# Attention layers: query and key projections earlier in periods 1, 2, 4 and 5, and another order of the weight splits where the two layers meet

## What is computed

```
x  = layernorm(x * s1)
q  = (x Wq^T) * qdc      k = (x Wk^T) * kdc      v = (x Wv^T) * vdc * s2
out  = softmax(q k^T / sqrt(32)) v          # 16 heads of 32, 128 tokens
y    = (out Ww^T) * wdc + (v Wu^T) * udc    # "W": output product, "U": skip product
dc[b, o] = 1 / sqrt(sum_i W[o, i]^2 s[b, i]^2 + 1e-8)
```

## Time and profile before

| | us |
|---|---|
| median of 3 runs | 4036.56 |
| lowest, highest | 4034.94, 4038.31 |
| profiled execution | 4034.65 |
| its span | 4032.3 |
| mean granted TensorE clock | 0.954 |

### The profile page before, as it was taken

One profiled execution on the slowest core, in us unless ns is written; L12 is line 12 of the kernel. 1 busy time (PEld: TensorE's weight loads), 2 busy tenths in 40 slices (PEclk: granted clock), 3 DMA queues, 4 the chain that ended last, 5 costly groups with the idle time before them and its releaser, 6 DMA issues. The chain is left out here.

```text
span 4032.3 us, 63692 instructions
## 1 busy us (share of the span) xinstructions
PE 3744.9 (93%) x22068; PEld 2296.2 (57%) x22068; DVE 3030.6 (75%) x3176; ACT 1335.1 (33%) x2014; POOL 1886.6 (47%) x1446
## 2 busy tenths in 40 slices
PE   8999759999998789999999999988999759999999
PEld 6777513333433567777767777756777513434344
DVE  4766679999996667777777777744666669999997
ACT  3555401111111444343434444323555401111111
POOL 2655635555553123344454444342555635555554
PEclk9999859999999799999999999998999959999999
DMA  3666755565654323222322222223666755556563
GB/s 121 241 239 239 298 178 167 179 194 173 196 176 125 101 87 122 79 81 81 106 87 90 79 79 79 66 80 116 229 240 246 271 189 166 189 179 194 172 193 120
DMA packets 272123, 630.17 MB, mean 156 GB/s; under 512 B 33216, under 2 KB 35904, under 8 KB 271840
## 3 DMA queue, kind: packets, MB, share of 16 engines
q1 hardware_dynamic: 267568, 619.03, 46.1%
q10 hardware_dynamic: 4352, 8.39, 0.6%
HBM read 390.87 MB, written 241.70 MB: 157 GB/s over the span
## 5 line engine op out<-in xcount | busy, mean ns | idle before, releaser
L1156 DVE CUSTOM_DVE_ANT_0 l3r_g<-l3r_g,l3r_pv,l3r_cf 128x1024 f32<-128x1024 f32 x512 | 674.5, 1339 | 70.8 <-PE l3r_pv L962 48.2
L1156 DVE CUSTOM_DVE_ANT_0 l0r_g<-l0r_g,l0r_pv,l0r_cf 128x1024 f32<-128x1024 f32 x512 | 674.1, 1339 | 69.4 <-PE l0r_pv L962 48.0
L102 PE MATMUL l1h_ps_p<-l1h_xh,l1c_wh 128*128 128x512 f32 x768 | 324.0, 422 | 9.2 <-POOL l1c_wl L2159 4.7
L104 PE MATMUL l1h_ps_p<-l1h_xl,l1c_wh 128*128 128x512 f32 x768 | 309.0, 402 | 0.0
L2120 POOL TENSOR_TENSOR l1h_st<-l1h_veps 128x1 f32<-128x1 f32 x64 | 35.4, 554 | 582.1 <-DVE l1h_veps L1983 582.1
L103 PE MATMUL l1h_ps_p<-l1h_xh,l1c_wl 128*128 128x512 f32 x768 | 306.5, 399 | 0.0
L974 PE MATMUL l3r_py<-l3r_g,l3r_cd 128*32 128x512 f32 x2048 | 283.0, 627 | 0.1
L962 PE MATMUL l0r_pv<-l0r_x,l0r_wv 32*128 32x512 f32 x1024 | 260.9, 508 | 23.2 <-POOL l0r_wv L882 15.6
L962 PEld LDWEIGHTS l3r_pv<-l3r_x,l3r_wv 32*128 32x128 f32 x1024 | 97.5, 188 | 324.4 <-issue 204.5
L962 PE MATMUL l3r_pv<-l3r_x,l3r_wv 32*128 32x512 f32 x1024 | 262.4, 512 | 21.1 <-POOL l3r_wv L882 15.8
L962 PEld LDWEIGHTS l0r_pv<-l0r_x,l0r_wv 32*128 32x128 f32 x1024 | 96.8, 186 | 324.2 <-issue 204.3
(11 more groups left out here) (386 smaller groups left out, 9038.4 us busy)
## 6 DMA issues: line engine op xcount, KB each, us to landing
l0r_x<-xhl_s SPq DMA_DIRECT2D x128, 512.0 KB, 11.7
l3r_x<-xhl_s SPq DMA_DIRECT2D x128, 512.0 KB, 11.2
xhl_s<-l0a_xo SPq DMA_DIRECT2D x116, 512.0 KB, 4.6
xhl_s<-l3a_xo SPq DMA_DIRECT2D x116, 512.0 KB, 4.6
gate_s<-l0a_gate SPq DMA_DIRECT2D x64, 256.0 KB, 2.7
l0r_dx<-dx_s SPq DMA_DIRECT2D x32, 512.0 KB, 13.3
l0r_gate<-gate_s SPq DMA_DIRECT2D x32, 512.0 KB, 13.9
l0r_crow<-feed_s SPq DMA_DIRECT2D x64, 256.0 KB
```

The lines of the kernel that those rows point to most:

```text
L102: pe.matmul(out, wh, xh, start=first, stop=False)
L104: return pe.matmul(out, wh, xl, start=False, stop=last)
L1156: dve._custom_dve(bass.dve_ops.TENSOR_ADD_SAT, out=g[:, t, j, :], in0=g[:, (t - 1) % TS, j, :], in1=pv[j % 2][:, :], s0=cf[:, q, t, 0, j:j ...
```

## The change

In periods 1 and 2 TensorE now does the Q projection ahead of values 0 (where U stands in later periods) and the K projection between turn 1 and values 1 (where W stands). In periods 4 and 5, where U exists, Q goes between turn 1 and values 1 and K stays. `jobs` lists the new order, so that the banks follow. VectorE's keep_q and ScalarE's keep_k move forward with them. Period 3, a burst, and all other periods keep their order.

In period 31 ScalarE makes the high half of K ahead of a normalise and of X2, and that of V ahead of the high halves of v and o. GpSimd makes the low half of K ahead of the low halves of v and o, and that of V ahead of the addition of W and the scaling of x.

```diff
--- before.py
+++ after.py
@@ -1341,9 +1341,17 @@
 
         def jobs(p):
             names = BURST if p.mod(4) == 3 else PLAIN
+            if extra(p) and p.off < 3:
+                return ("Q", "K", "S", "T", "V", "U", "W")
+            if extra(p) and p.off > 3:
+                return ("U", "Q", "S", "K", "T", "V", "W")
             if extra(p):
                 names = names[:-3] + ("Q", "S", "K", "T", "V")
             return names
+
+        def sooner(p, job):
+
+            return extra(p) and p.off != 3 and (p.off < 3 or job == "Q")
 
         def bank(p, name):
 
@@ -1662,19 +1670,27 @@
                 if p.is_at(0):
                     sum_rows(3)
                     sum_rows(4)
+                if sooner(p, "K"):
+                    project(p, Q, "Q", q_mm)
                 values(g, 0)
                 turn(g, 1)
                 if burst:
                     turn_x(p, "X3")
                 mix_w(p)
+                if sooner(p, "K"):
+                    project(p, K, "K", k_mm)
+                elif sooner(p, "Q"):
+                    project(p, Q, "Q", q_mm)
                 values(g, 1)
                 turn(g, 2)
-                project(p, Q, "Q", q_mm)
+                if not sooner(p, "Q"):
+                    project(p, Q, "Q", q_mm)
                 if extra(p):
                     next_sum_rows(p)
                 values(g, 2)
                 turn(g, 3)
-                project(p, K, "K", k_mm)
+                if not sooner(p, "K"):
+                    project(p, K, "K", k_mm)
                 if extra(p):
                     next_add_rows(p)
                 values(g, 3)
@@ -1787,10 +1803,10 @@
                 keep_pt(g, 0)
                 if burst:
                     high_x(p, "X1")
+                    if p.is_at(B - 1):
+                        high_swap(K)
                     normalise(p.plus(4))
                     high_x(p, "X2")
-                if p.is_at(B - 1):
-                    high_swap(K)
                 exponent(p, 0)
                 for m in range(5):
                     if p.is_at(m + 1):
@@ -1818,17 +1834,20 @@
                     take_root(root, skip, 3)
                     high_weight(3)
                     square_weight(3)
+                if p.is_at(B - 1):
+                    high_swap(V)
                 high_v(p.plus(-3))
                 high_o(p.plus(-5))
-                if p.is_at(B - 1):
-                    high_swap(V)
+                if sooner(p, "K"):
+                    keep_k(p)
                 keep_pt(g, 2)
                 keep_pt(g, 3)
                 if p.is_at(B + 3):
                     high_swap(U)
                 if p.is_at(B + 5):
                     high_swap(W)
-                keep_k(p)
+                if not sooner(p, "K"):
+                    keep_k(p)
                 keep_o(g)
                 keep_v(p)
                 if p.is_at(-1):
@@ -2052,6 +2071,8 @@
                 if burst:
                     low_x(p, "X1")
                 centre(p, 0)
+                if sooner(p, "K"):
+                    keep_q(p)
                 scale_u(p)
                 if burst:
                     low_x(p, "X2")
@@ -2067,6 +2088,8 @@
                 if burst:
                     low_x(p, "X3")
                 scale_w(p)
+                if sooner(p, "Q") and not sooner(p, "K"):
+                    keep_q(p)
                 if p.is_at(-1):
                     pair_factor()
                     keep_skip()
@@ -2082,7 +2105,8 @@
                 if p.is_at(B - 1):
                     low_swap(Q)
                 share(p, 0)
-                keep_q(p)
+                if not sooner(p, "Q"):
+                    keep_q(p)
                 if extra(p):
                     spill_next(p)
                 if p.is_at(4):
@@ -2169,14 +2193,14 @@
             def period(p):
                 factors(p.plus(4))
                 add_u(p.plus(-4))
+                if p.is_at(B - 1):
+                    low_swap(K)
                 low_v(p.plus(-3))
                 low_o(p.plus(-5))
                 if p.is_at(B - 1):
-                    low_swap(K)
+                    low_swap(V)
                 add_w(p.plus(-6))
                 scale_x(p.plus(5))
-                if p.is_at(B - 1):
-                    low_swap(V)
 
             periods(pool, LEAD, TAIL, period)
```

## The result

The changed kernel takes 4014.16 us (median of 13 runs, 4009.23 to 4023.29) against 4033.06 us (13 runs, 4023.07 to 4038.31) for the kernel before on the same chips: a ratio of 0.9958, 95% interval 0.995 to 0.9965, or 17 us less (14 to 20). The profiled execution took 4014.11 us, its span is 4011.8 us. Runs of one kernel spread over 14 to 15 us here, so stretches of a trace say more about single steps than totals do. The two profiled executions differ by more than the ratio says, by 20.5 us (4034.65 to 4014.11); 16.6 of them lie between period 1's scores and the phase's last scores, and the rest outside, where the change touches nothing.

What follows compares the result with a forecast made beforehand. TensorE, busy 93% of the span, was taken as the bound, losing time only to waits and the lower clock. Wins of 5.4 + 2.8 + 0.3 + 1.4 + 5.0 = 14.9 us off 4036.56 gave 4021.7 us, range 4014 to 4029.

Steps and rivals of the forecast that it cites:

- The stands: Periods 1, 2, 4, 5: TensorE's 4.76 us waits ahead of values 1 go in periods 1 and 2; others remain, up to 3.0.
- The clock's charge: Periods 1 and 2: 0.5 and 1.3 us added for TensorE running at the lower clock after the new stands.
- Period 5: Falls from 25.50 to 24.1 us: stands of 3.0 and 1.4, plus 1.4 for the lower clock; 1.4 won.
- The sum: Periods 1, 2, 4, 5 and the joint: 5.4 + 2.8 + 0.3 + 1.4 + 5.0 = 14.9 us won.
- The joint: Period 31: three waits become one of some 3.5 us ahead of Q; stretch 27.4 us, 5.0 won (1.5 to 6.5).
- Rival 2: Joint: GpSimd keeps the port through its next two copies, so little is won there; 4025.2 us, chance 0.13.
- Costed at nothing: Period 3's kept order, bank waits in periods 4 to 6, keep_q and SyncE's loads: each 0, or 0.5 us at most.
- Rival 1: Early periods: the waits only move and the clock is lost again, giving 3 us for 9.9; 4028.6 us, chance 0.12.
- Rival 3: Early periods: several short stands each bring back the lower clock, making the kernel slower, 4045 us at 120 matmuls; chance 0.03.
- the sign of 0.85: Early periods: clocks under 0.85 there would show the forecast wrong.
- Rival 4: All changed periods: the clock stays up everywhere, 21.3 us won, 4015.3 us; chance 0.07.

Runs made afterwards that it cites:

- three queue experiments: Changed kernel with one move each: VectorE's period 2 row factors later (4013.02 us), ScalarE's period 4 square root later (4008.11), next layer's row factors earlier (4008.31).
- early kernel: Changed kernel with the joint's orders of ScalarE and GpSimd put back, so only periods 1, 2, 4 and 5 change: 4022.93 us, ratio 0.9971.
- repeat: The changed kernel once more, unaltered: 4013.53 us (1 run).
- root: Changed kernel with ScalarE's square root of period 4 behind pt 2 (its copy for values 2) instead of ahead: 4008.11 us (1 run).
- next row factors: Changed kernel with the next layer's row factors on VectorE behind period 4's second share instead of at its end: 4008.31 us (1 run).
- low Q moved: Changed kernel with VectorE's low Q at the joint right behind X2's low half, before GpSimd's low K: 4015.14 us (1 run).
- low Q and low V moved: Changed kernel with VectorE's low Q behind X2's low half and GpSimd's low V right behind low K: 4010.64 us (1 run).
- all five moves: Changed kernel with period 2 row factors, square root and next row factors moved, low Q first, low V behind low K: 4002.46 us, ratio 0.9927.
- GpSimd alone: Kernel before with only GpSimd's two moved splits at the joint, ScalarE in its old order: 4036.16 us (1 run); joint 27.04 us.

## Why the prediction was right, step by step

- **The stands.** Right: values 1 without a stand in periods 1 and 2; 2.56 (2.7 forecast) ahead of T in period 2; 2.35 (2.65) ahead of values 2 in period 4; 2.86 (3.0) ahead of values 1 in period 5. The short ones were put too high: 1.2 ahead of values 2 in periods 1 and 2 was 0.58 in each, and 0.7 ahead of T in period 1 was 0.51. The three queue experiments show the causes of the long ones. TensorE's work without waits was put too low: 15.3 us in period 1, where it was busy for 15.86, and 18.3 in period 4, where it was busy for 18.57 at the full clock. The two errors nearly cancel. (The forecast's sums take 1.8 us for the two stands of period 1 and 3.95 for those of period 2, where their terms add up to 1.9 and 3.9.)
- **The clock's charge** is the term that was mis-sized most. 0.5 and 1.3 us were put on periods 1 and 2; in the profiled execution they lost nothing. Of the six other profiles with period 2's order unaltered, five (the early kernel, the repeat, and those with root, next row factors or low Q moved) put period 2 at 21.0 to 22.0, and only the one with low Q and low V moved at 19.45. So for period 2 the charge was a fair mean, and the profiled execution was lucky. Period 1 took 16.94 to 16.96 us in every profile of the new order: its 0.5 was wrong.
- **Period 5** was charged twice, for a second stand of 1.4 and for the lower clock. The lower clock stretched turn 2 and S (1.94 us for a busy 1.07) just where TensorE would have stood, and no stand was left: 22.85 in place of 24.1. The 24.1 would have been met by other terms: in the two executions in which period 4 had kept the full clock with its stand of 2.35, the lower one lasted in period 5 into the key projection, and the period took 24.00 and 24.04 us (0.86), without a second stand.
- **The sum.** Over periods 1 to 5 the new order took 105.96 to 109.44 us in the five profiles that have it unaltered (the change, its repeat, the early kernel and the two with low Q moved), mean 107.30, and the old one 119.11 to 119.85 in four, mean 119.38: 12.1 us won on average, where 9.9 were forecast. The joint's order gives 26.69 on average where 27.4 was forecast. Against the 32.42 before, the two averages add up to 17.8 us, inside the 14 to 20 measured. So the forecast was short by about 2 us in the early periods and 0.7 at the joint.
- **The joint.** Right in mechanism and nearly in size (27.4 forecast; 25.69 to 27.71 in the six profiles that have its order unaltered): one wait of 3.5, low Q of 3.70, low V ended ahead of V. In the changed kernel's profile the lower clock lasted through Q, 5.26 us where 4.5 were put, and left K at the full one, where 0.6 were put. Rival 2 (GpSimd keeps the port) is out: when low K ended at 2002.94, VectorE, which had been waiting, went first, and GpSimd's low half of v, 1.27 us alone, took 3.34. GpSimd's order alone is worth 5.4 (32.42 - 27.04), ScalarE's 0.3.
- **Costed at nothing.** Period 3 took 24.31 us for 24.14 (its second stand is 2.54 for 2.17), and period 7 25.47 for 24.03, by a lower clock behind an unchanged stand of 2.50 (0.93 for 1.00). Of the 18.2 won in five stretches 16.6 are left between period 1's scores and the phase's last ones (1265.4 us for 1282.0).
- **Rival 1** (the waits only move) holds for period 4 alone, 0.2 won, and there only with the lower clock: at the full one the same order won 1.75 (22.66 - 20.91).
- **Rival 3** (slower by the clock) is out: the worst of the five profiles above still won 9.7 us in periods 1 to 5 (119.11 - 109.44). That one has the only clock under the sign of 0.85 in a period that the change touches, 0.84 in period 2 (21.99 us), 2.5 us more than at the full level; in the changed kernel's own two profiles no early period is under 0.92.
- **Rival 4** (the clock stays up everywhere, 4015.3 us) has the number nearest to the measured one, by chance: its mechanism did not hold. The clock was 0.92 in period 4, 0.93 in period 5 and 0.88 at the joint.

## What to carry to other kernels

Where an engine in strict order stands behind another's queue, work put into the hole wins the hole, and the next stand is read from the same queue's next entries; here the long ones could be told to 0.3 us, the short ones to 0.6. Before moving an operation of GpSimd with two SBUF operands forward, list which ones of VectorE will be queued against it, since each waited for the other whole here (3.70 us for 2.28, 6.66 for 4.5). Filling a pause of some 2 to 3 us won the pause or, by luck, some 1.5 us more, so one profile is too few to size such a step.

## What the hardware showed that was not expected

The same stand of TensorE brought the lower clock in some executions and not in others. For one and the same program this shows in period 2, which took 19.45 us (clock 1.00) or 21.05 (0.92) after the same 2.56, and at the joint, 27.60 (0.88) or 25.69 (1.00) after the same 3.5. Across kernels that have the same order there it shows too: after 2.35 in period 4 22.45 us or 20.91, and after 2.50 in period 7 25.47 or 24.03. Even 3.5 us at the joint left the clock at 1.00 in two of six profiles, while 2.03 us in period 5 of the kernel with all five moves was followed by 0.92.

The price was 1.4 to 1.6 us in periods 2, 4 and 7 as a rule and up to 2.0 at the joint; 2.5 (period 2, 21.99) and 2.7 (period 7 of GpSimd alone, 26.72) were seen once each. With the stand of period 4 at 0.61 us in place of 2.35 that period was at the full clock in both kernels that did so, but so it was in two kernels that kept the 2.35. What decides between the two outcomes stays open.
